# First maxima of an attention taken as lower half plus excess, a shorter look-ahead, and wide exponentials at the end

## The reference, cut to what matters

```
query = heads(...) + heads(rope(...));  key = ... ;  value = ...
attn = jnp.einsum('bhqd,bhkd->bhqk', query, key) / scale
attn = jax.nn.softmax(attn, axis=-1)
out = jnp.einsum('bhqk,bhkd->bhqd', attn, value)
```

## Time and profile before

| what | value |
|---|---|
| runs | 1263.73, 1259.1, 1263.58 us; median 1263.58 |
| profiled execution, first to last instruction (span) | 1167.0 us |
| what the median has beyond that span | 96.6 us |
| TensorE busy | 1050.2 us, 90% |
| VectorE busy | 947.4 us, 81% |
| ScalarE busy | 780.1 us, 67% |
| GpSimd busy | 330.1 us, 28% |
| mean granted TensorE clock | 0.951 |

### The profile page before, as it was taken

One profiled execution on the slowest core, in us unless ns is written; L12 is line 12 of the kernel. 1 busy time (PEld: TensorE's weight loads), 2 busy tenths in 40 slices (PEclk: granted clock), 3 DMA queues, 4 the chain that ended last, 5 costly groups with the idle time before them and its releaser, 6 DMA issues. The chain is left out here.

```text
span 1167.0 us, 23760 instructions
## 1 busy us (share of the span) xinstructions
PE 1050.2 (90%) x9028; PEld 497.3 (43%) x9028; DVE 947.4 (81%) x1447; ACT 780.1 (67%) x1559; POOL 330.1 (28%) x467
## 2 busy tenths in 40 slices
PE   6987699586778999999999999999999989988997
PEld 4786599443421222222222222222222229657755
DVE  7976555478789999999999999999999908965555
ACT  4543434144422999999999999999999994543421
POOL 4732367667520000000000000000000007347472
PEclk9998899898775999999999999999999999999998
DMA  7011267319980022210222012220220000423322
GB/s 242 1 37 37 87 204 201 108 34 209 203 221 1 3 35 35 34 28 10 35 35 35 17 21 35 35 34 4 34 35 3 2 2 2 154 82 96 95 71 74
DMA packets 94151, 76.81 MB, mean 66 GB/s; under 512 B 42932, under 2 KB 73012, under 8 KB 93528
## 3 DMA queue, kind: packets, MB, share of 16 engines
q1 hardware_dynamic: 89176, 65.33, 24.1%
q0 software_dynamic: 4864, 9.97, 3.4%
HBM read 47.74 MB, written 27.46 MB: 64 GB/s over the span
## 5 line engine op out<-in xcount | busy, mean ns | idle before, releaser
L1464 DVE TENSOR_REDUCE mx<-p_psA 128x1 f32<-128x1024 f32 x512 | 585.3, 1217 | 9.3 <-PE p_psA L1627 9.3
L1555 ACT ACTIVATE p_pt<-p_psS 128x512 f32<-128x512 f32 x1024 | 548.3, 597 | 37.8 <-PE p_psS L1649 18.2
L1662 PE MATMUL p_acc<-p_pt,V 128*32 128x256 f32 x4096 | 328.4, 392 | 15.5 <-ACT attn L1546 13.8
L1627 PE MATMUL p_psA<-K,Q 48*128 48x512 bf16 x1024 | 319.7, 394 | 9.4 <-DVE mx L1464 7.8
L1649 PE MATMUL p_psS<-Q,K 51*128 51x512 bf16 x1024 | 309.9, 384 | 0.0
L1662 PEld LDWEIGHTS p_acc<-p_pt,V 128*32 128x32 f32 x4096 | 81.9, 108 | 211.1 <-ACT p_pt L1555 110.5
L1381 POOL TENSOR_TENSOR mr<-zeros,mx 128x16 f32<-128x16 f32 x32 | 7.1, 222 | 547.1 <-DVE mx L1464 547.1
L1627 PEld LDWEIGHTS p_psA<-K,Q 48*128 48x128 bf16 x1024 | 57.1, 94 | 232.8 <-DVE mx L1464 197.8
L1649 PEld LDWEIGHTS p_psS<-Q,K 51*128 51x128 bf16 x1024 | 62.5, 93 | 18.1 <-ACT p_pt L1555 12.6
L1069 DVE TENSOR_TENSOR f_h<-f_bank,b 128x512 f32<-128x512 f32 x40 | 27.7, 692 | 38.4 <-PE f_bank L1137 38.4
L1029 ACT ACTIVATE f_h1T<-f_h 128x512 f32<-128x512 f32 x40 | 25.1, 629 | 31.4 <-DVE f_h L1069 31.4
(11 more groups left out here) (343 smaller groups left out, 1447.0 us busy)
## 6 DMA issues: line engine op xcount, KB each, us to landing
f_w<-in_w SPq DMA_DIRECT2D x40, 256.0 KB, 3.4
Q<-q_rows SPq DMA_DIRECT2D x32, 192.0 KB, 4.7
K<-k_rows SPq DMA_DIRECT2D x32, 192.0 KB, 5.3
hrows<-h SPq DMA_DIRECT2D x8, 512.0 KB, 3.2
result<-f_shared_kept SPq DMA_DIRECT2D x11, 256.0 KB
result<-f_y SPq DMA_DIRECT2D x10, 256.0 KB, 3.6
V<-v_rows SPq DMA_DIRECT2D x16, 144.0 KB, 5.7
x<-in_x SPq DMA_DIRECT2D x4, 512.0 KB, 5.2
```

The lines of the kernel that those rows point to most:

```text
L1464: dve.tensor_reduce(mx[v % 2][:, h, qt:qt + 1], psA[t][:], AX.X, ALU.max).then_inc(a_max, 1)
L1555: act.activation(pt[s % 2][:, head_at(s, j), :], psS[k % 3][:], ACT.Exp, scale=INV_SCALE).then_inc(s_out, 1)
L1627: mm = pe.matmul(psA[t][:, c * 512:(c + 1) * 512], Q[g % NBUF][rows, pair, q0:q0 + P], K[g % NBUF][rows, pair, c * 512:(c + 1) * 512], sta ...
L1662: mm = pe.matmul(acc[VW * h:VW * (h + 1), cols], V[g % NBUF][:, kc, h * (HD + 1):h * (HD + 1) + VW], pt[s % 2][:, h, cols], start=(kc == 0 ...
```

## The change

Four things are edited.

1. The first unit's sixteen row maxima (steps 0 to 7, FAST = 8) are made in another way. TensorE makes the difference of the upper and the lower half of the row (upper scores, then scores with negated keys `nk` added in the same bank) and the lower half by itself. ScalarE takes relu of the difference into `excess` (SBUF). VectorE adds lower and excess and takes the maximum in one instruction over 512 columns, `tensor_tensor_reduce`. Four slots of banks are used (`lower`, `upper`), from `psA`, `psS` and `acc`. The negated keys come from two VectorE operations over 48 partitions and 1024 columns.
2. AHEAD is 12 instead of 13, for all units. TURN stays 4.
3. From step WIDE0 = 246 on (the last ten), the scores go into `psA`, two heads beside each other, and ScalarE takes exponentials 1024 columns wide, two to a step instead of four.
4. The waits of the first steps follow from these.

```diff
-AHEAD = 13
+AHEAD = 12
+FAST = KC
+SLOTS = 4
+WIDE0 = NSTEPS - AHEAD + 2
+        nk = pt[0][:, 0, :].bitcast(BF16).rearrange("p (c t) -> p c t", c=2)
+        excess = [pt[1][:, i, :] for i in range(SLOTS)]
+        lower = [psA[0][:, 0:512], psA[1][:, 0:512], psS[0][:], psS[2][:]]
+        upper = [psA[0][:, 512:L], psA[1][:, 512:L], psS[1][:], acc[:]]
...
-                for s in range(NSTEPS):
+                dve.wait_ge(group_in[0], GROUP_IN)
+                for r in range(2):
+                    rows = slice(64 * r, 64 * r + KROWS)
+                    dve.tensor_scalar(nk[rows, :, :], K[0][rows, :, 0:512], -1.0, None, ALU.mult).then_inc(nk_ready, 1)
+                for s in range(FAST):
+                    for t in range(2):
+                        i, h, qt = 2 * s + t, 2 * (s // 4) + t, s % 4
+                        dve.wait_ge(a_mm, i + 1)
+                        dve.wait_ge(r_ready, i + 1)
+                        dve.tensor_tensor_reduce(out=excess[i % SLOTS], in0=lower[i % SLOTS], in1=excess[i % SLOTS], scale=1.0, scalar=-3.0e38,
+                                                 op0=ALU.add, op1=ALU.max, accum_out=mx[0][:, h, qt:qt + 1]).then_inc(a_max, 1)
+                for s in range(FAST, NSTEPS):
...
+                def above(i):
+                    act.wait_ge(d_mm, i + 1)
+                    if i >= SLOTS:
+                        act.wait_ge(a_max, i - SLOTS + 1)
+                    act.activation(excess[i % SLOTS], upper[i % SLOTS], ACT.Relu).then_inc(r_ready, 1)
+                for i in range(2 * FAST):
+                    above(i)
                 turned(0)
...
-                    for j in range(QUAD):
+                    for t in range(2 if s >= WIDE0 else 0):
+                        act.wait_ge(w_mm, 2 * (s - WIDE0) + t + 1)
+                        act.activation(pt[s % 2][:, 2 * t:2 * t + 2, :].rearrange("p h t -> p (h t)"), psA[t][:], ACT.Exp,
+                                       scale=INV_SCALE).then_inc(w_out, 1)
+                    for j in range(0 if s >= WIDE0 else QUAD):
...
+                def first_difference(s, t, part):
...
+                        pe.matmul(upper[i % SLOTS], q, high, start=True, stop=False)
...
+                    pe.matmul(upper[i % SLOTS], q, minus_low, start=False, stop=True).then_inc(d_mm, 1)
+                def first_lower(s, t):
...
+                    if i >= SLOTS:
+                        pe.wait_ge(a_max, i - SLOTS + 1)
+                    pe.matmul(lower[i % SLOTS], q, low, start=True, stop=True).then_inc(a_mm, 1)
...
+                def wide_scores(s, t):
...
+                    if i < 2:
+                        pe.wait_ge(a_max, 2 * NSTEPS)
+                    else:
+                        pe.wait_ge(w_out, i - 1)
+                    for r in range(2):
+                        rows = slice(64 * r, 64 * r + KROWS + MROWS)
+                        mm = pe.matmul(psA[t][:, r * 512:(r + 1) * 512], K[g % NBUF][rows, t, kc * P:(kc + 1) * P],
+                                       Q[g % NBUF][rows, t, half * 512:(half + 1) * 512], start=True, stop=True)
+                    mm.then_inc(w_mm, 1)
...
-                for s in range(AHEAD):
+                for s in range(FAST):
+                    for part in range(2):
+                        for t in range(2):
+                            first_difference(s, t, part)
+                    for t in range(2):
+                        first_lower(s, t)
+                for s in range(FAST, AHEAD):
                     for t in range(2):
                         a_part(s, t, 0)
                         a_part(s, t, 1)
-                    if s == KC:
-                        pe.wait_ge(full_ready[1], NM)
+                    if s == FAST:
                         turn(0)
                 for s in range(NSTEPS + 1):
+                    if s >= WIDE0:
+                        for t in range(2 if s < NSTEPS else 0):
+                            wide_scores(s, t)
+                        for part in range(2):
+                            values(s - 1, part)
+                        continue
```

More of the change, by code:

```diff
@@ L1258, in phase_project_attention1 @@
         at_step = n.sem("at_step")
+        nk_ready, d_mm, r_ready = n.sem("nk_ready"), n.sem("d_mm"), n.sem("r_ready")
+        w_mm, w_out = n.sem("w_mm"), n.sem("w_out")
         Q, K, V, mp = M.Q, M.K, M.V, M.mp
@@ L1617, in a_part @@
                     q0, rows = (half * 4 + qt) * P, slice(64 * t, 64 * t + KROWS)
-                    if w == 0 and t == 0 and c == 0:
+                    if w == 0 and t == 0 and c == 0 and g >= 1:
                         pe.wait_ge(group_in[g % NBUF], (g // NBUF + 1) * GROUP_IN)
[L1620 to L1626, removed]
+                    if c == 0:
+                        pe.wait_ge(a_max, 2 * (s - 1) + t + 1 if s > FAST else 2 * s + t - SLOTS + 1)
                     mm = pe.matmul(psA[t][:, c * 512:(c + 1) * 512], Q[g % NBUF][rows, pair, q0:q0 + P],
@@ L1630, in a_part, with first_operands @@
                         mm.then_inc(a_mm, 1)
+                def first_operands(s, t):
+                    pair, q0, rows = s // 4, (s % 4) * P, slice(64 * t, 64 * t + KROWS)
+                    return Q[0][rows, pair, q0:q0 + P], K[0][rows, pair, 0:512], K[0][rows, pair, 512:L], nk[rows, pair, :]
+                def first_difference(s, t, part):
+                    i = 2 * s + t
+                    q, _, high, minus_low = first_operands(s, t)
+                    if part == 0:
+                        if i >= SLOTS:
+                            pe.wait_ge(r_ready, i - SLOTS + 1)
+                        elif i == 0:
+                            pe.wait_ge(group_in[0], GROUP_IN)
+                            pe.wait_ge(full_ready[0], NM)
+                        elif i == 1:
+                            pe.wait_ge(ct_ready, NM)
+                            pe.wait_ge(v_out, NM)
+                        elif i == 2:
+                            pe.wait_ge(full_ready[1], NM)
+                        pe.matmul(upper[i % SLOTS], q, high, start=True, stop=False)
+                        return
+                    if i < 2:
+                        pe.wait_ge(nk_ready, i + 1)
+                    pe.matmul(upper[i % SLOTS], q, minus_low, start=False, stop=True).then_inc(d_mm, 1)
+                def first_lower(s, t):
+                    i = 2 * s + t
+                    q, low, _, _ = first_operands(s, t)
+                    if i >= SLOTS:
+                        pe.wait_ge(a_max, i - SLOTS + 1)
+                    pe.matmul(lower[i % SLOTS], q, low, start=True, stop=True).then_inc(a_mm, 1)
                 def turn(v):
@@ L1651, in scores @@
                               start=True, stop=True).then_inc(s_mm, 1)
+                def wide_scores(s, t):
+                    g, half, kc, i = s // GSTEPS, (s % GSTEPS) // KC, s % KC, 2 * (s - WIDE0) + t
+                    if kc == 0 and t == 0:
+                        pe.wait_ge(m_in[half], (g + 1) * 32)
+                    if i < 2:
+                        pe.wait_ge(a_max, 2 * NSTEPS)
[6 more added lines that the diff above has]
+                    mm.then_inc(w_mm, 1)
                 def values(s, part):
                     g, kc = s // GSTEPS, s % KC
-                    if part == 0:
+                    if part == 0 and s >= WIDE0:
+                        pe.wait_ge(w_out, 2 * (s - WIDE0) + 2)
+                    elif part == 0:
                         pe.wait_ge(s_out, score_at(s, QUAD - 1) + 1)
```

## The result

The changed kernel took 1273.13 us (median of 6 runs, 1268.98 to 1274.87), the kernel before 1263.65 (6 runs beside them, 1259.1 to 1266.23). The ratio is 1.0074, 95% interval 1.0055 to 1.0092: slower by 7.0 to 11.6 us. The forecast was slower, 1278.2 us, range 1265 to 1286. The direction and the deciding term were right; the sum was 3 to 8 us too high.

What follows compares the result with a forecast made beforehand. TensorE was taken to set the loop's pace, with VectorE and ScalarE nearly full. Terms -4.5 - 2.35 + 0.1 + 23.2 - 1.8 = +14.65 us, added to 1263.58, gave 1278.2 us, range 1265 to 1286.

Steps and rivals of the forecast that it cites:

- the deciding term: Transposes of the next unit's maxima in the loop: TensorE waits, net 0.75 us each, 31 times, 23.2 us lost.
- first unit: Ahead of the loop, the first unit's maxima made the new way end at 352.2 instead of 356.70: 4.5 us gained.
- one step ahead of the loop: With look-ahead 12 the loop starts one step of two reductions earlier: 2.35 us gained.
- wide exponentials: In the tail, 1024-column exponentials follow each other at 0.96 us, 1.95 us a step instead of 2.13: 1.8 us gained.
- clock (a rival): Dense first unit raises TensorE's clock earlier, so the loop's first half steps gain 2.6 us: 1275.6 us, chance 0.18.
- step more with maxima in the tail: One tail step more still carries maxima and takes 2.21 instead of 2.13 us: 0.1 us lost.
- Nothing later gives it back: Loop behind each transpose's wait: half steps are full and the `acc` wait follows the same stall, so 23.2 us stays lost.
- hidden or a half absorbed stall: Rivals on the transposes' wait: slack hides it, 1255 us, chance 0.12; or absorbs half, 1266 us, chance 0.08.
- the fused instruction: First unit's add and maximum on VectorE: 0.69 us each, between 0.61 and 0.78; slow rival 1.01, 1283 us, chance 0.10.
- the negations were hidden: Ahead of the first unit, VectorE's two key negations end before ScalarE reaches relu; unhidden they cost up to 2.4 us.
- TensorE sets the pace: In the loop, TensorE's own work fills a half step of 1.11 us, so any time its list stands is paid by all.
- the 96.6 us around the span: Whole program: the median before, 1263.58 us, was taken as the profiled span of 1167.0 us and 96.6 us around it.

Runs made afterwards that it cites:

- e4: Changed kernel with look-ahead 13 and no wide steps, so the new first unit alone, against the kernel before: ratio 0.9955.
- e2: Kernel before with look-ahead 12 and nothing else changed: 1287.66 us, ratio 1.0178 to the kernel before.
- e8: Kernel before with four more small GpSimd operations ahead of each split of the maxima, 1.2 us later: ratio 1.003 to before, one run.
- e9: Kernel before with eight more small GpSimd operations ahead of each split of the maxima, 2.4 us later: ratio 1.027 to before, one run.
- e3: Changed kernel, look-ahead 12, with the transpose issued behind the second half of the values: 1259.68 us, ratio 0.9968 to the kernel before.
- e6: Changed kernel, look-ahead 12, with the transpose later still, behind the next step's first piece of maxima: ratio 0.9951 to the kernel before.
- e10: Changed kernel with look-ahead 13, plus unread fill matmuls between first unit and loop, 6 behind each pair of pieces: ratio 0.9946 to the kernel before.
- e1: Changed kernel with the look-ahead put back to 13, the rest kept: 1256.87 us, ratio 0.9932 to the kernel before.
- e7: Changed kernel, look-ahead 12, with the transpose moved to step 5 of each unit (TURN = 5): ratio 0.9987 to the kernel before.
- e11: Changed kernel with look-ahead 13, plus unread fill matmuls between first unit and loop, 10 behind each pair of pieces: ratio 0.9979 to the kernel before.

## Why the prediction came out so

In the stretch the difference divides like this, each from marks in the two profiles of before and after:

| term | forecast | measured | from |
|---|---|---|---|
| first unit | -4.5 | -5.6 | last key operation to GpSimd's start: 356.70 - 337.15 = 19.55, then 360.71 - 346.76 = 13.95 |
| one step ahead of the loop | -2.35 | -2.4 | from there to the first exponential: 11.80, then 9.39 |
| waits ahead of the transposes | +23.2 | +22.8 | GpSimd's start from unit 1 to 31: 554.43, then 576.48, and one more 0.75 |
| wide exponentials | -1.8 | -2.4 | the rest of the tail; -2.55 alone |
| clock (a rival) | 0 | -0.9 | the loop's first steps |
| step more with maxima in the tail | +0.1 | in the tail's row | |
| sum | +14.65 | +11.5 | |

The measured terms of the wide exponentials and of the clock come out of marks that one step of 2.22 us has shifted. From the first exponential to unit 1's split it is 9.57 us before and 10.87 after, 1.30 = 2.22 - 0.92. From the last split to the last copy of `acc` it is 29.35 and 25.48 us, -3.87 = -2.22 + 0.75 - 2.4.

The mechanism and the deciding term were right. The sum was 3.15 us too high because four terms, each off by 0.4 to 1.1 us, were all off to the same side; one of them, the clock, has no shown cause.

- The deciding step held to a hundredth: the transpose's half step was to grow by 0.77 + 0.06 = 0.83 us and grew by 2.11 - 1.27 = 0.84; net 0.75 forecast, 19.21 - 18.46 = 0.75 measured. It was read wholly from before: where the transpose had once waited for GpSimd gave the length of the chain, the loop gave its slack, and one step gave the shift. Over all units it is a little less, (576.48 - 554.43) / 30 = 0.735, since a few units before were 0.1 us longer than the rest.
- "Nothing later gives it back" held. The rivals with a hidden or a half absorbed stall fall: the look-ahead alone costs 21.9 us.
- The mis-sized term was the fused instruction. I took 0.69, the middle of 0.61 and 0.78; it is 0.61, because the accumulator read costs no time of its own. Fifteen distances, each 0.08 us shorter, are 1.2 us, about the 1.1 that the forecast missed. The Trainium skill (VectorE: DVE Perf Modes, "Two Vector instructions with no wait between them") says that an operation which also writes out its accumulator is two instructions, and this trace agrees: the read is a row of its own, 0.08 us long. But it starts together with the next main instruction, so my inference from two instructions, nearer 0.78, was wrong.
- TensorE and ScalarE did feed it, and the negations were hidden, as forecast.
- That TensorE sets the pace was read from the tail's rows as "nothing waited for"; one of those rows names ScalarE (0.41 us, as long as where the next one names `issue`). The 1.10 us of the half step behind the stall, which ends at `issue`, bears the reading out.
- The wide exponentials lay beyond my bound: the pace is 0.951 us and not 0.96, and TensorE's round did not hold it up.
- The clock rival was right that the clock rises in the dense first unit, and wrong in what it gives: it fell again before the loop. At look-ahead 13 the loop's exponentials reach full pace (no more waits between them) 8.1 us after the first one, both before and with the new first unit (8.1 and, in e4, 7.9). At look-ahead 12 it is 6.0 to 6.4 us in the four kernels with the new first unit (6.0 in the changed one) and 10.3 in e2, the one without it. Lengthening the split alone (e8, e9) gives 6.4 and 6.0. So the 0.9 us is not shown to come from the first unit.
- The text on the 96.6 us around the span was wrong, as told above; no term rested on it.

The version that beats both kernels is the change with the look-ahead of 13, 0.7% faster than before and 1.4% faster than the change (0.9932 / 1.0074). No other version beats it: e3, e4, e6 and e10 overlap it in the intervals of their ratios, but their stretches are 2.4 to 4.4 us longer.

## What to carry to other kernels

- A look-ahead is not only a depth of buffers. Find each consumer that hangs on the last of the looked-ahead work, take its slack from the trace (when it could have started against when it did), and compare it with the length of one step. Here 1.45 us of slack met a shift of 2.22, 31 times.
- An engine whose list is full pays for a wait in full, and so do those behind it (0.75 us a unit here). If work must become later, move its consumer back in the list, but not between two matmuls that start together (0.48 us lost here), and not so far that a DMA trip behind it, whose time varies (1.4 to 3.5 us here), loses its slack.
- Take parts apart before judging the whole: two of the three were gains, together 0.7%, and the third hid them.

## What the runs showed of the hardware that was not expected

- The instruction that reads VectorE's accumulator lasts 0.08 us and starts together with the next fused instruction, so a fused add and maximum over 512 columns with its [128, 1] result goes at 0.61 us each (the changed kernel, 351.38 - 350.76 and on).
- The same program took 1262 to 1265 us on the chips of e1 to e7 and 1166.5 us on that of e8 to e11. Its profile on one of the slower chips has three waits of together 92.6 us in the last feed-forward stage. No run here says why.
- In e10 the clock fell to 1.2 GHz near 352 us, with fill matmuls ahead of and behind the fall, and the granted clock stayed at 0.50 from 355 to 365 us, in which TensorE was busy the whole time. What would have kept it stays open.
- The landing in DRAM of one and the same small transfer, `m_rows<-p_mT`, let the next one be issued 1.37 us later in most units of e7 and 3.45 us later in one.
- A 128x128 transpose between two matmuls that start together on different rows of the array costs 0.47 us (e6, 1.58 against 1.11 us for the half step), three times as much as in front of the values (0.16 us).
